# A four-layer kernel on one core: the second batch's balancing moved to ACT and PE in logarithms, and the binary weights' preparation moved into the first projection

## What is computed

```python
def sinkhorn_log(logits, num_iters=50, tau=0.1):
    Z = logits / tau
    def step(carry, _):
        u, v = carry
        u = -logsumexp(Z + v[..., None, :], axis=-1)
        v = -logsumexp(Z + u[..., :, None], axis=-2)
        return ((u, v), None)
    (u, v), _ = scan(step, (0, 0), None, length=50)
    return exp(Z + u[..., :, None] + v[..., None, :])
```

## Time and profile before

| | us |
|---|---|
| median of 3 runs | 1462.56 (1456.24 to 1465.91) |
| the profiled execution | 1467.78 |
| its span, first to last instruction | 1466.1 |
| busy in the span: PE, DVE, ACT, POOL | 1113.0, 871.3, 577.3, 320.6 |
| mean granted clock of PE | 0.868 of 2.4 GHz |

### The profile page before, as it was taken

The page is one execution under the profiler, slowest core; times in us unless marked ns, Lnnn a source line. Parts: engine busy times, 40 slices in busy tenths (PEclk is TensorE's granted clock), DMA queues, the critical chain, the costliest instruction groups (busy, mean ns, idle before and its releaser), DMA issues.

```text
span 1466.1 us, 20210 instructions
## 1 busy us (share of the span) xinstructions
PE 1113.0 (76%) x7526; PEld 456.1 (31%) x7526; DVE 871.3 (59%) x1773; ACT 577.3 (39%) x785; POOL 320.6 (22%) x514
## 2 busy tenths in 40 slices
PE   2769999895788639746555457878788988898887
PEld 1444444342233314312312111222222233333332
DVE  4212222003666679886888988657758577746663
ACT  2413333000554435126113246574445555434452
POOL 1114444004841102001011043700010032111220
PEclk9869999997899859677776768998879999999999
DMA  3421220003210001100200111411002110210100
GB/s 130 144 87 45 85 65 22 0 0 94 65 29 18 12 1 55 34 6 20 62 13 22 56 53 36 138 29 31 17 27 74 50 32 23 77 54 28 53 18 29
DMA packets 53590, 67.14 MB, mean 46 GB/s; under 512 B 9494, under 2 KB 43412, under 8 KB 53488
## 3 DMA queue, kind: packets, MB, share of 16 engines
q1 hardware_dynamic: 49516, 55.95, 12.5%
q0 software_dynamic: 3984, 9.98, 2.4%
HBM read 46.82 MB, written 18.82 MB: 45 GB/s over the span
## 4 chain that ended last, share of the span: by engine, by line
PE 36%; DVE 31%; ACT 5%; issue 4%; SPq 1%; DMA 1%; ACTq 0%; DVEq 0%
DVE w_mx L1388 13%; PE w_banks L653 10%; PE w_po L1303 9%; PE w_banks L1285 4%; PE w_banks L1257 4%; DVE w_region L1875 3%; PE w_banks L1245 2%; ACT w_pr L1331 2%; DVE w_region L1872 2%; DVE w_region L1853 2%; DVE w_region L1870 2%; PE w_banks L1313 2%; PE w_banks L1539 1%; DVE w_region L1868 1%; DVE w_region L1866 1%
## 5 line engine op out<-in xcount | busy, mean ns | idle before, releaser
L1388 DVE TENSOR_REDUCE w_mx<-w_banks 128x2 f32<-128x1024 f32 (+3 forms) x352 | 377.1, 1087 | 195.6 <-PE w_banks L1257 194.0
L1331 ACT ACTIVATE w_pr<-w_banks 128x1024 f32<-128x1024 f32 (+1 forms) x312 | 315.1, 1013 | 429.3 <-PE w_banks L1285 427.9
L1370 POOL TENSOR_SCALAR_AFFINE_SELECT w_pr<-w_pr 128x512 f32<-128x512 f32 (+1 forms) x184 | 104.7, 569 | 561.5 <-ACT w_pr L1331 561.3
L1285 PE MATMUL w_banks<-w_qs,w_ks 49*128 49x512 f16 (+7 forms) x832 | 137.1, 354 | 91.1 <-DVE w_mx L1388 60.0
L1257 PE MATMUL w_banks<-w_ks,w_qs 48*128 48x512 f16 (+7 forms) x832 | 144.8, 361 | 40.9 <-DVE w_mx L1388 23.1
L1303 PE MATMUL w_po<-w_pr,w_vz 128*17 128x512 f32 (+7 forms) x1152 | 155.1, 565 | 12.7 <-ACT w_ou L1353 12.7
L78 PE MATMUL f_pp<-xt,sl_region 128*128 128x512 f16 x672 | 149.1, 382 | 3.5 <-POOL sl_region L492 3.5
L1245 PE MATMUL w_banks<-mask_half,ident_half 64*128 64x128 bf16 (+1 forms) x768 | 67.0, 254 | 37.2 <-DVE w_mx L1388 16.8
L78 PEld LDWEIGHTS f_pp<-xt,sl_region 128*128 128x128 f16 x672 | 65.1, 98 | 84.8 <-issue 5.6
L466 DVE TENSOR_TENSOR sl_region<-sl_region,f_pp 128x512 f32<-128x512 f32 x28 | 19.3, 688 | 121.3 <-ACT sl_region L481 121.3
L1285 PEld LDWEIGHTS w_banks<-w_qs,w_ks 49*128 49x128 f16 (+1 forms) x832 | 41.8, 99 | 138.9 <-issue 57.5
(11 more groups left out here) (223 smaller groups left out, 1533.6 us busy)
## 6 DMA issues: line engine op xcount, KB each, us to landing
stack_scratch<-sl_region SPq DMA_DIRECT2D x102, 128.0 KB
w_qs<-stack_scratch SPq DMA_DIRECT2D x96, 96.0 KB, 2.3
sl_region<-in_L_gu SPq DMA_DIRECT2D x14, 512.0 KB
w_stage<-in_L_w POOLq DMA_DIRECT2D x36, 128.0 KB, 2.4
sl_region<-in_L_down SPq DMA_DIRECT2D x14, 256.0 KB
stack_scratch<-p_qk SPq DMA_DIRECT2D x24, 128.0 KB
w_ks<-stack_scratch SPq DMA_DIRECT2D x32, 96.0 KB, 2.6
bw_stage<-in_L_w SPq DMA_DIRECT2D x4, 640.0 KB, 6.0
```

What stands on the lines that cost most here:

```text
L1285: mm = pe.matmul(g.banks.pair_at(f)[:, half, at:at + T - q0], g.ks[base:base + self.rows + 1, k_slot, k_place, j * P:(j + 1) * P], g.qs[ba ...
L1331: act.activation(g.probs.at(self.pr_fill[s])[:, :, 0:width], g.banks.pair_at(self.s_fill[s])[:, :, 0:width], ACT.Exp, scale=self.a.scale). ...
L1370: pool.affine_select(out=diagonal, in_=diagonal, compare_op=ALU.is_ge, fill=0.0, base=0, pattern=pattern, channel_multiplier=-1).then_inc( ...
L1388: dve.tensor_reduce(out, g.banks.pair_at(self.m_fill[m])[:, :, 0:heads * keys].rearrange("q h (p k) -> q h p k", k=keys), AX.X, ALU.max).t ...
```

## The change

1. **`LogStreams`, a subclass of `Streams`, for s1 alone.** The logits go by PE into a PSUM bank, transposed so that the 16 entries of a matrix lie on partitions. Each half round (rows, or columns; 100 in all) is four ticks: ACT takes `Exp` of the bank (`h_e`), PE multiplies it with a constant f32 128x128 matrix that sums by rows or columns (`totals`), ACT takes `Ln` of the sums (`h_l`), PE subtracts that, with a third constant matrix, from the logits in the bank. Each waits for the one before it. DVE does no balancing for s1. A last `Exp` and two transposes bring the matrix back. s0 is balanced as before.
2. **The cuts.** s0 is cut at balancing tick 100 (180 before), s1 at balancing tick 40 (of 400; 60 of 300 before), and its ticks from balancing tick 280 on, with the mixing, move beside a20, at the head of the strand of o11.
3. **ACT's tables.** Behind each `Sqrt` and `Silu` of the woven part an explicit load of the table set `natural_log_exp_and_others` is issued.
4. **First part.** The binary weights are loaded in the phase of `norm_and_split`, behind its own loads, and a second time in their natural layout (10 blocks of 128 rows). In `project`, ACT takes two signs behind each of the first four steps and one absolute value, with its sum (`accum_out`), behind each of the ten. PE has 5 matmuls left to spread the row scales, DVE a handful of small instructions. SP loads the first two slabs of `swiglu_low_rank` at the start of this phase.

```diff
-    def signs(self, act):
+    def sign(self, act, c):
+        n = self.n_qk + self.n_v
         act.wait_ge(self.w_here, 16 * KC)
-        for c in range(KC):
-            n = self.n_qk + self.n_v
-            act.activation(self.sign_qkv[:, c, :], self.stage[:, c, 0:n], ACT.Sign)
-            act.activation(self.sign_o[:, c, :], self.stage[:, c, n:], ACT.Sign).then_inc(self.signed, 1)
-        for c in range(KC):
-            act.wait_ge(self.signed, c + 1)
-            act.activation(self.stage[:, c, :], self.stage[:, c, :], ACT.Abs).then_inc(self.absd, 1)
+        act.activation(self.sign_qkv[:, c, :], self.stage[:, c, 0:n], ACT.Sign)
+        act.activation(self.sign_o[:, c, :], self.stage[:, c, n:], ACT.Sign).then_inc(self.signed, 1)
+
+    def magnitude(self, act, k):
+        act.wait_ge(self.n_here, 32)
+        act.activation(self.by_row[:, k, :], self.by_row[:, k, :], ACT.Abs,
+                       accum_out=self.mean[:, k:k + 1]).then_inc(self.absd, 1)
...
-            binary.signs(act)
+                if n < KC:
+                    binary.sign(act, n)
+                binary.magnitude(act, n)
...
-            binary.load(sp)
+            for u in range(2):
+                load_slab(sp, ins, slabs, u, u, g.slab_here[u])
...
+class LogStreams(Streams):
...
+        k, hop = divmod(t - self.bal_at, 4)
+        if 0 <= k < self.halves and hop == 1:
+            pe.wait_ge(self.entries.sem, self.entries.at + k + 1)
+            pe.matmul(banks.at(self.fills["totals"])[:, 0:64], self.sums[:, k % 2, :], g.h_e[:, :],
+                      start=True, stop=True).then_inc(self.totals.sem, 1)
+        if 0 <= k < self.halves and hop == 3:
+            pe.wait_ge(self.logs.sem, self.logs.at + k + 1)
+            pe.matmul(banks.at(self.fills["logs"])[:, 0:64], self.sums[:, 2, :], g.h_l[:, :],
+                      start=False, stop=True, skip_group_check=True).then_inc(self.taken.sem, 1)
...
+                act.wait_ge(self.taken.sem, self.taken.at + k)
+            act.activation(g.h_e[:, :], banks.at(self.fills["logs"])[:, 0:64], ACT.Exp, scale=self.INV_TAU)\
+                .then_inc(self.entries.sem, 1)
+        if 0 <= k < self.halves and hop == 2:
+            act.wait_ge(self.totals.sem, self.totals.at + k + 1)
+            act.activation(g.h_l[:, :], banks.at(self.fills["totals"])[:, 0:64], ACT.Ln).then_inc(self.logs.sem, 1)
...
-        cut = s0.bal_at + 180
+        cut = s0.bal_at + 100
...
-        s1 = Streams(g, 1, sl[:, 1], w24, wb, base24[:, :], gate[:, :], n11, [])
+        s1 = LogStreams(g, 1, sl[:, 1], w24, wb, base24[:, :], gate[:, :], n11, [small.done()], sums)
...
-        cut1 = s1.bal_at + 60
+        cut1, cut2 = s1.bal_at + 40, s1.bal_at + 280
...
-               [some_of(s1, cut1, s1.ticks[-1] + 1)], [all_of(split2)]],
+               [some_of(s1, cut1, cut2)], [all_of(split2)]],
...
-        merge([[body_of(a20)], [all_of(o11), all_of(n21), all_of(p21), all_of(r20), lead_of(a21)], [all_of(split3)]],
+        merge([[body_of(a20)], [some_of(s1, cut2, s1.ticks[-1] + 1), all_of(o11), all_of(n21), all_of(p21), all_of(r20),
+                                lead_of(a21)], [all_of(split3)]],
```

183 lines of the change are left out of this document (136 added, 47 removed).

## The result

The changed kernel takes 1580.54 us (median of 4 runs, 1569.97 to 1583.97) against 1464.24 us of the kernel before (4 runs): a ratio of 1.0791, 95% interval 1.0720 to 1.0862. That is 116 us slower (110 between the two profiled spans). The forecast was 44 us slower, with 1550 as the upper end of its range: the sign is right, the size is far off. The profiled execution took 1577.37 us, its span 1575.7, at a mean granted clock of 0.827 (0.868 before).

A forecast was written before the change was run, and what follows sets the result against it. DVE, filled by the balancing, was taken to set a11's end, with two engines close together in a01 and a20. The terms -19 - 17 + 9 + 26 + 45 = +44 gave 1507 us, range 1440 to 1550 for 8 in 10.

The forecast's parts named there:

- The first part: Before the second phase: ACT's share hides beside the projection, next phase starts at 73 instead of 94; -19 us, bounds -22 and -10.
- a10: Body a10: 42 more balancing steps, 11.8 us on DVE, three quarters of it counted; +9 us, bounds +2 and +12.
- The unit price: One half round of the chain, two matmuls, two ACTIVATEs, four hops: 1.5 us at full clock, 2.15 at the low one.
- PE's own 61.1 us are 57, and 5 for waits that remain: In a11: PE's existing work shrinks to 57 us at clock 0.75, plus 5 us for normalisation and DMA waits.
- 127 x 0.27/0.75 = 46: In a11: the chain's 127 matmuls keep PE 0.27 us each at full clock, taken at clock 0.75; 46 us.
- 74 waits x 0.54 = 40: In a11: 74 chain matmuls directly behind another make PE wait 0.54 us each for the ACT turn; 40 us.
- they are costed at nothing: In a20: the 44 mixing instructions moved there, 15 us of DVE, add nothing; up to 15 us if cover is gone.
- 73 x 0.27/0.85 = 23: In a20: the chain's 73 matmuls keep PE 0.27 us each at full clock, taken at clock 0.85; 23 us.
- The low clock, much slower: Rival: 1.2 GHz in a11 and a20 brings both near their upper bounds; 1570 us half way there; chance 0.07.
- PE kept busy, faster: Rival: added matmuls hold PE's clock high in a11 and early a20, a11 -5, a20 +5; 1436 us; chance 0.18.
- The exposures counted twice: Rival: half the direct waits fall where PE waits anyway, a11 +8, a20 +20; 1464 us, no change; chance 0.13.
- three signs named for a wrong forecast: Half round with nothing between clearly under 1.5 us, a11 under 135 us, or a20 growing by under 20.

The follow-up runs named there:

- The fillers: Changed kernel with one, then two, unused f16 matmuls of 448 columns behind each matmul of the chain: 1544.98 us, then 1534.23 us.
- two fillers: Changed kernel with two unused f16 matmuls of 448 columns behind each matmul of the chain: 1534.23 us, ratio 1.0491.
- The multiplications on POOL: Kernel with only the first part changed, the second batch's 100 balancing multiplications moved from DVE to POOL: 1452.13 us, ratio 0.9954.
- bf16 and fillers: Changed kernel with the chain in bf16 (one pass a matmul) and one unused f16 matmul behind each: 1495.52 us, ratio 1.0251.

## Why the forecast was wrong in size

In the profiled spans, 44 us forecast have become 110. Of the 66 us between, a20 has 43, a11 10, a10 5, the first part 3, a01 1, and what comes behind a20, which was costed at nothing, 3.

**The first part** (-19 forecast, -15.7 at the end of a00) and **a01** (-17 forecast, -15.8) came about as worked out. The second phase's first matmul is 21.9 us earlier, for 21 forecast. The first part alone brings the whole kernel 11 us; 5 to 9 us of it are lost again, and where is not settled.

**a10** (+9, bounds +2 to +12) measured +13.7. With the chain left out it is +11.8 (133.8 us), the full price of its 42 steps and not three quarters; the chain's first five matmuls, which run from 699.0 us on at its end, make the rest. (The cut puts ten half rounds into a10's order, but in time they run in a11.)

**The unit price** was right. 2.15 and 1.5 us a half round forecast, 2.00 and 1.50 measured. The `Exp` and `Ln` took 0.223 us where the forecast had 0.25. The Trainium skill (ScalarE: Activation LUTs, Rules for kernel authors) gives about 0.3 us and 0.83 ns an element for an ACTIVATE whose bias is a `[128,1]` pointer operand, an estimate of 0.35 us here. The forecast left that condition out, and the calls of the chain name no bias. From 128x64 (0.223 us) to the attention's 128x1024 (1.023 us before the change) the traces agree on the 0.83 ns an element, with 0.17 us where the page has 0.3. On the tables its section "Table sets: the hidden batching unit" agrees with the trace: in the 264 us of the chain ACT loads a table set twice, both at the `Sqrt` of the normalisation (782.4 and 783.9 us), and at no other turn between an `Exp` and an `Ln`. In all there are 35 loads against 32, the three more that were counted, and taking the explicit ones away changed nothing.

**a11** was 154 in the forecast and is 164.3; that it came near is luck, since errors offset each other. The step "PE's own 61.1 us are 57, and 5 for waits that remain" gave 62; with the chain left out the body takes 79.4, PE busy 55.3 and idle 24. The step "127 x 0.27/0.75 = 46" measured 73.4 busy, 0.58 us each: the clock was 0.61 instead of 0.75, and a matmul that waits for its input occupies PE for 0.69, not 0.54. The step "74 waits x 0.54 = 40", with 6 behind exponentials, was too high: PE's idle time is 32.0 with the chain and 24.1 without it, since much of the chain's waiting replaces waiting that was there, and part of what I had counted as waiting is busy time in the profile's account.

**a20** was +45 and is +88, and this is where the forecast broke. Its 88.4 us are 60.7 more busy and 27.7 more idle on PE (179.1 and 64.9 against 118.4 and 37.2). Two steps failed. With the chain left out 58.7 of the 88.4 us go and 29.7 stay, where the forecast had 45 and nothing.

The first step, and by this order of removal the larger miss, is "they are costed at nothing", of the 44 mixing instructions. With the chain left out the body is still 29.7 us longer than before; with the mixing put back it is 161.8. The forecast looked at DVE's occupancy ("128 of some 200 us"), but the mixing stands at the head of the strand that holds the outward projection, the next normalisation and projection. The 15 us set as the price if the cover is gone was also too low: a20 gives back 23.5 us, and the whole kernel 17. With the chain in place, moving both back only moved the time (412.2 against 408.3 us), so the two shares can't simply be added.

The second is the clock, "73 x 0.27/0.85 = 23". In the first 112 us of a20, while the chain runs, the clock is 0.59 and the chain's matmuls keep PE busy 43.8 us:

```profile
868.30:980.00 111.70, 21.55 (x69) 15.64 (x69) 0.59 0.03 9
...
868.30:980.00 111.70, 22.27 (x70) 16.22 (x70) 0.59 0.03 9
```

(The same stretch twice, of L1955 alone and of L1959 alone.) They are 0.63 us each instead of the 0.32 of the forecast. PE's other work is slower too: in a20 it is 179.1 - 43.8 = 135.3 us, 17 more than before, for nearly the same matmuls. The forecast priced this old work as if it were untouched. But 10 of the 17 are there without the chain as well (128.1 us busy, at 0.79), so some 7 come with it. The chain's 58.7 us are thus 43.8 of its own matmuls, 7 of slowed old work and 8 more of idle time, where the forecast had 23, nothing, and 22 for waits that the body's own idle time did not absorb: what it took too low for the clock it had in part taken too high for the waits. The fillers show that the clock is cause and not company: with nothing changed but more work on PE, the clock rose and 35 and then 46 us went away, 30 and 40 of them in a11 and a20.

**The rivals.** "The low clock, much slower" (1570, given 0.07) is nearest in time and names the right place, but its parts did not come so. a20 is at its upper bound (+88.4; +87 for "the low clock wherever the chain runs and the mixing exposed", a sum that the prediction doesn't show), and a11, at 164.3, is far below its bound of 206. Nor does 1570 follow from half way in the two bodies: 52 and 66 us there give 1554. "PE kept busy, faster" decided from 0.95 in a11; two fillers reach 0.99 there, and the kernel is still 1534 us, so a high clock alone does not make the chain pay. "The exposures counted twice" was right about a11's waits, but not about the time. And none of the three signs named for a wrong forecast appeared: all of them looked for a chain that costs too little, none for one that costs too much.

**The first paragraph of the forecast** said that DVE sets a11's end. The multiplications on POOL qualify it: 23 us less work on DVE, and no gain. The length of the balancing's chain bounded a11 too, and not DVE's occupancy alone. That chain had hops of 0.03 us within one engine; the changed one turns between two engines four times a half round.

No kernel tried with the balancing on PE and ACT beats the one before. Even bf16 and fillers leave it at 1495. The first part alone beats the kernel before, by 0.8 to 1.0%.
